# First mixture of experts of a four-layer decoder in blocks of 128 rows, with the rows as the stationary operand, four weight buffers and eight PSUM banks

## The chip, the cores and the metric

The kernel is one program on one core of a Trainium2 chip. The metric is device time in microseconds, the median of three runs. The profile and the trace are from one further execution.

## The reference, cut to what matters

A decoder of four layers works on x of 8 x 256 tokens with 256 features (2048 tokens, f32). Twelve stages follow one another; ten of them are not touched in their arithmetic or their order. The stage that is rewritten is the feed-forward part of layer 0, a mixture of 8 experts of which each token takes two:

```python
logits = jnp.einsum('th,eh->te', xf, w_router)
topw, topi = jax.lax.top_k(jax.nn.softmax(logits, axis=-1), 2)
topw = topw / jnp.sum(topw, axis=-1, keepdims=True)
gate = jax.nn.silu(jnp.einsum('th,eih->eti', xf, w_gate))   # 8 experts, i = 704, h = 256
up = jnp.einsum('th,eih->eti', xf, w_up)
down = jnp.einsum('eti,ehi->eth', gate * up, w_down)
out = jnp.einsum('eth,te->th', down, combine)               # combine holds topw at topi
```

A second stage matters for one part of the change: the self-attention of layer 3, which has a learned score for each distance between two tokens.

## The kernel before

Each stage is a class, and emits its whole instruction order for the five queues (PE, ACT, DVE, POOL, SP). An engine's queue runs in the order in which it is written; every wait is a semaphore wait in that order. `Uses` hands out PSUM banks (8 banks of 512 f32 columns) in rotation: `take` makes PE wait until the bank's last contents were copied out. By default it rotates over banks 0 to 5. Banks 6 and 7 are used by `Norm` for the turned activations (L389 to L405) of the next stage, four groups of four tiles each, whose transposes are issued while the present stage ends.

**The mixture, `L0Mixture`.** The router picks two experts for each token, which gives 4096 rows. Rows of one expert are put into blocks of BLOCK = 256 rows, no block holds two experts, and the program runs the largest number of blocks that can be needed: (4096 + 8 x 255) // 256 = 23. Empty places in a block are computed all the same; the scatter leaves them out. For block j:

- SP reads the expert's number and loads its whole weights (gate, up and down, 128 partitions x 4352 f32, 2176 KB) into one of RING = 3 buffers (L1357 to L1362). The load of block j waits for the last product of block j - 3.
- POOL gathers the rows with two indirect DMAs of 128 rows (L1169), into one of two buffers.
- PE turns the rows (`pe_turn`, 4 transposes), multiplies gate and up, 6 tiles of the 704 hidden features, with weights as the stationary operand and 256 rows as the moving one (24 products, L221), turns the rows of block j + 1, and then makes the down product of block j (12 products, L1283). An f32 product shows as two instructions.
- For each tile ACT takes silu of gate (L1298) and DVE multiplies by up (L1326), which gives the hidden features already turned as the down product wants them. ACT copies the result out (L1304), and POOL scatters it with two indirect DMAs (L1176).

The order on POOL is what sets when rows arrive:

```python
def pool(self):
    self.load_rows(0)
    self.load_rows(1)
    for j in range(BLOCKS):
        self.load_rows(j + 2)
        pool.wait_ge(*self.uses.emptied(self.y_use[j]))
        ...  # scatter of block j
```

So the gather of block j + 3 comes behind the scatter of block j in POOL's queue, and that scatter waits for the copy of the down product of block j.

**The distances in `L3Attention`.** For 8 batches, 2 tiles and 2 halves of the features (32 areas) PE makes 4 products into 4 banks (L2858), DVE and ACT copy two banks each (L236, L231) into one of 4 slots, and SP stores the slot to DRAM as `positions` (L2928): 1024 KB for each of 16 areas, 512 KB for each of the other 16, 25.2 MB in all. A slot is written again when its store has landed. When all are stored, SP loads the positions back (L2920), skewed; PE goes on with the queries and values and needs the first of them at the attention's first score.

Of the kernel before, what the change touches and what calls it, by code (L numbers as in the profile page):

```python
# [17 lines left out]
P = 128  # L18
# [9 lines left out]
BLOCK = 256  # L28
# [60 lines left out]
class Uses:  # L89
# [4 lines left out]
    def __init__(self, k, first=0, count=6):  # L94
        self.k, self.first, self.count, self.at = k, first, count, 0
        self.table, self.counts = [], {"dve": 0, "act": 0, "sums": 0}
# [1118 lines left out]
class L0Mixture(Mixture):  # L1215


    RING = 3

    def __init__(self, k):  # L1220
# [3 lines left out]
        MT = self.MT = tiles_of(I)  # L1224
        self.BT = BLOCK // P
# [4 lines left out]
        s4, s5, s6 = k.slab[4], k.slab[5], k.slab[6]  # L1230
        self.rows = [s4[:, 512 * n:512 * n + 512].rearrange("p (a c) -> p a c", a=2) for n in range(2)]
        self.rowsT = [s4[:, 1024 + 512 * n:1536 + 512 * n].rearrange("p (c t) -> p c t", c=DC) for n in range(2)]
        self.y = [s4[:, 2048 + 512 * n:2560 + 512 * n].rearrange("p (a c) -> p a c", a=2) for n in range(2)]
        self.silu = [s4[:, 3072 + 256 * n:3328 + 256 * n] for n in range(4)]
        self.hid = [s[:, 0:MT * BLOCK].rearrange("p (m t) -> p m t", m=MT) for s in (s5, s6)]
# [14 lines left out]
        self.rows_shared(self.BT, BLOCKS)  # L1250

    def pe_turn(self, j):
        k, nc, use = self.k, self.k.nc, self.uses
        if j < BLOCKS:
            k.pe.wait_ge(*self.rows_in(j))
            bank = use.take(self.turn[j])
            for c in range(DC):
                for a in range(2):
                    t = nc.tensor.transpose(bank[:, BLOCK * c + P * a:BLOCK * c + P * a + P],
                                            self.rows[j % 2][:, a, P * c:P * c + P], k.ident)  # L1260
# [2189 lines left out]
```

## Time and profile before

| what | value |
|---|---|
| median of 3 runs | 2955.96 us (2955.13 to 2957.3) |
| the profiled execution, its time | 2950.55 us |
| its span from first to last instruction | 2949.3 us |
| mean granted TensorE clock | 0.917 |
| PE busy | 2515.4 us, 85% of the span |
| mixture of layer 0, from the first gate product to the last down product | 257.46 to 651.30 us |
| distances of layer 3, from the first product to the first query product | 2215.33 to 2288.55 us |

A granted clock of 1.00 is 2.4 GHz, one of 0.50 is 1.2 GHz. Times in the rows are microseconds from the start of the span. The span leaves out what lies around it, 1.25 us in the profiled execution.

### The profile page before, as it was taken

Reading aid. Unit: us, or ns where it says so; the run is one execution under the profiler, and the core shown is the slowest. Engines: PE = TensorE matmul, PEld = TensorE weight load, DVE = VectorE, ACT = ScalarE, POOL = GpSimd, SP = SyncE. Lnnn points to the kernel's source line nnn. Section 1 sums busy time; section 2 is a strip of 40 time slices with the busy share of each in tenths; the row PEclk is TensorE's granted clock in tenths of the full one; section 3 lists DMA queues with packets and bytes.
Section 4 is the critical chain, followed back from the end, with each engine's and each line's share of the span. In section 5 each row is a group of like instructions: output and inputs, shape, how many; then the busy total and the mean of one; then the engine's idle time right before and its main releaser. Section 6 shows DMA issues by size and latency. Waiting matters only on the chain.

```text
span 2949.3 us, 34538 instructions
## 1 busy us (share of the span) xinstructions
PE 2515.4 (85%) x13798; PEld 1737.2 (59%) x13798; DVE 1221.9 (41%) x2235; ACT 870.2 (30%) x2379; POOL 570.1 (19%) x566
## 2 busy tenths in 40 slices
PE   4876999985899587887899999699956999867999
PEld 4764777764676363423566667577732788733555
DVE  6553111118588563556233321300044355665220
ACT  1110111113475161454222221122213344313220
POOL 2521222215201001211344310222220100012000
PEclk8977999997999798998899999699976999988999
DMA  4003443422001000300000000323227323100000
GB/s 149 1 29 139 174 160 145 169 79 78 1 2 48 0 2 0 119 1 29 1 0 0 1 1 14 110 83 96 71 88 313 158 87 130 37 25 0 8 8 15
DMA packets 73751, 189.50 MB, mean 64 GB/s; under 512 B 9551, under 2 KB 52949, under 8 KB 65654
## 3 DMA queue, kind: packets, MB, share of 16 engines
q1 hardware_dynamic: 65590, 169.11, 15.9%
q0 software_dynamic: 8000, 18.18, 1.9%
q8 instruction: 109, 1.79, 0.3%
q14 instruction: 52, 0.43, 0.0%
HBM read 143.88 MB, written 46.09 MB: 64 GB/s over the span
## 4 chain that ended last, share of the span: by engine, by line
PE 49%; DVE 6%; issue 1%; ACT 1%; POOL 1%; DMA 1%; SPq 0%; POOLq 0%; DVEq 0%; ACTq 0%
PE psum L221 25%; PE psum L3140 6%; PE psum L1685 3%; PE psum L2183 2%; PE psum L2170 2%; PE psum L3149 2%; PE psum L1680 2%; PE psum L2858 1%; PE psum L1696 1%; PE psum L1711 1%; DVE stats L253 1%; DVE arena L2230 1%; PE psum L2400 1%; POOL small L2598 1%; PE psum L404 1%
## 5 line engine op out<-in xcount | busy, mean ns | idle before, releaser
L221 PE MATMUL psum<-arena 128*128 128x256 f32 (+6 forms) x4112 | 994.3, 401 | 24.7 <-DVE arena L3236 13.5
L221 PEld LDWEIGHTS psum<-arena 128*128 128x128 f32 (+3 forms) x4112 | 718.9, 182 | 288.4 <-issue 147.4
L1770 DVE TENSOR_REDUCE small<-psum 128x4 f32<-128x1024 f32 (+1 forms) x112 | 137.0, 1223 | 152.8 <-PE psum L1685 108.6
L263 POOL TENSOR_SCALAR x_moments<-x_moments 128x4 f32<-128x4 f32 x48 | 12.0, 250 | 942.0 <-DVE x_moments L256 941.5
L1326 DVE TENSOR_TENSOR arena<-arena,psum 128x256 f32<-128x256 f32 x138 | 57.9, 420 | 317.7 <-ACT arena L1298 316.4
L1176 POOL DMA_INDIRECT l_out<-arena,slot_tables x86 | 85.6, 995 | 496.8 <-ACT arena L1304 287.8
L3140 PE MATMUL psum<-arena 128*128 128x512 bf16 x768 | 166.4, 379 | 0.0
L1745 ACT ACTIVATE arena<-psum,small 128x128 f32<-128x128 f32 (+1 forms) x384 | 148.9, 417 | 46.0 <-DVE small L1770 46.0
L1781 DVE COPY arena<-psum 128x512 f32<-128x512 f32 x224 | 143.5, 681 | 1.7 <-PE psum L1696 1.5
L404 PE MATMUL psum<-ident,z 128*128 128x128 f32 x256 | 47.0, 345 | 109.1 <-DVE z L274 79.7
L1745 ACT ACTIVATE z<-psum,small 128x128 f32<-128x128 f32 (+1 forms) x256 | 103.8, 425 | 117.6 <-DVE small L1770 117.6
L1283 PE MATMUL psum<-arena 128*128 128x256 f32 x552 | 136.5, 392 | 0.0
L1680 PE MATMUL psum<-arena 32*128 32x128 f32 (+1 forms) x1280 | 131.4, 336 | 0.0
L3140 PEld LDWEIGHTS psum<-arena 128*128 128x128 bf16 x768 | 75.2, 98 | 90.5
L2598 POOL TENSOR_TENSOR small<-small,minus_half 128x16 f32<-128x16 f32 x32 | 92.8, 2901 | 179.5 <-DVE small L2512 179.5
L221 PE MATMUL psum<-zT,arena 128*128 128x512 f32 x240 | 112.9, 625 | 7.2 <-DVE zT L234 5.7
L1283 PEld LDWEIGHTS psum<-arena 128*128 128x128 f32 x552 | 97.2, 189 | 32.8 <-issue 23.3
L2728 ACT ACTIVATE arena<-psum,small 128x269 f32<-128x269 f32 x128 | 61.4, 485 | 184.1 <-PE psum L221 171.8
L330 ACT ACTIVATE z<-x,x_shift,x_moments 128x256 f32<-128x256 f32 x96 | 52.2, 593 | 213.6 <-POOL x_shift L271 213.5
L1680 PEld LDWEIGHTS psum<-arena 32*128 32x128 f32 x1280 | 92.5, 189 | 38.6 <-issue 35.2
L221 PE MATMUL psum<-arena,zT 128*128 128x8 f32 (+2 forms) x384 | 108.6, 433 | 5.9 <-ACT zT L230 3.2
L1298 ACT ACTIVATE arena<-psum 128x256 f32<-128x256 f32 x138 | 52.7, 382 | 199.3 <-PE psum L221 197.9
(332 smaller groups left out, 3554.9 us busy)
## 6 DMA issues: line engine op xcount, KB each, us to landing
arena<-L_ffn_w_in SPq DMA_DIRECT2D x23, 2176.0 KB, 9.0
arena<-L_ffn_W_in SPq DMA_DIRECT2D x16, 1024.0 KB
positions<-arena SPq DMA_DIRECT2D x16, 1024.0 KB, 4.0
arena<-positions SPq DMA_DIRECT2D x16, 1024.0 KB, 7.9
arena<-l_out SPq DMA_DIRECT2D x16, 512.0 KB, 8.3
positions<-arena SPq DMA_DIRECT2D x16, 512.0 KB, 4.6
arena<-positions SPq DMA_DIRECT2D x16, 512.0 KB, 8.7
l_out<-arena SPq DMA_DIRECT2D x2, 2048.0 KB, 14.0
```

The source lines that it names most:

```text
L221: last = nc.tensor.matmul(out, lhsT, rhs, start=(n == 0), stop=(n == len(pairs) - 1))
L404: t = nc.tensor.transpose(bank[:, P * j:P * j + P], src[:, P * c:P * c + P], k.ident)
L1176: k.nc.gpsimd.indirect_dma_start(out=dram[:, :], out_offset=bass.IndirectOffsetOnAxis(ap=self.router.choice[0:count, n:n + 1], axis=0), in ...
L1283: mm = nc.tensor.matmul(bank[:, D * a:D * a + D], self.hid[j % 2][0:M, m, P * a:P * a + P], self.down[j % self.RING][0:M, m, :], start=(m ...
L1680: mm = nc.tensor.matmul(bank[:, at:at + L], self.q[p][strip, c, P * t:P * t + P], self.kT[strip, c, P * keys[0]:P * keys[0] + L], start=Fa ...
L1685: mm = nc.tensor.matmul(bank[:, at + P * a:at + P * a + P], self.positions(t, a, head), k.ident, start=False, stop=True, skip_group_check= ...
L1745: e = nc.scalar.activation(buf[:, at:at + L], src[:, at:at + L], ACT.Exp, bias=self.minus_top(h)[:, i:i + 1], scale=1.0, accum_out=self.su ...
L1770: nc.vector.reduce_max(self.minus_top(h), use.bank(u).rearrange("p (h l) -> p h l", l=L), AX_X, negate=True).then_inc(self.topped.up(), 1)
L1781: nc.vector.tensor_copy(self.turned[h % 4][:, 512 * s:512 * s + 512], use.bank(u)).then_inc(use.empties(u), 1)
L2598: k.nc.gpsimd.tensor_tensor(inv, inv, k.minus_half, ALU.pow).then_inc(self.inverted.up(), 1)
L2728: nc.scalar.activation(self.hid[e % 2][:, m, span], use.bank(u)[:, 0:self.half], ACT.Gelu, bias=self.b1[:, e, m:m + 1]).then_inc(use.empti ...
L3140: mm = nc.tensor.matmul(bank, self.w1[:, c, P * m:P * m + P], p[:, c, :], start=(c == 0 and n == 0), stop=(c == MT - 1 and n == 2))
```

## The change

The blocks of the first mixture have 128 rows, so there are (4096 + 8 x 127) // 128 = 39. For gate and up the turned rows are the stationary operand and 352 of the 704 weight columns the moving one: two halves of 4 products each, gate in one bank and up in the next. The hidden features come out with a row on each partition, so they are turned by 6 more transposes (`pe_hidden`), copied out by ACT (4 tiles) and DVE (2 tiles), and only then are they the stationary operand of the down product (6 products). The PE order is shifted: in its iteration j it makes the first half of block j, turns the hidden features of block j - 1, makes the second half of j, turns the rows of block j + 1, and makes the down product of j - 1. A block has one gather and one scatter in place of two each. There are four weight buffers. `Uses` rotates over all eight banks by default, in every stage that names no banks of its own (the cosine stage of layer 2 did already).

```diff
@@ -25,7 +25,7 @@
 LN_EPS = 1e-5
 SLAB = 4096
 ARENA = 9 * SLAB - 1024
-BLOCK = 256
+BLOCK = 128
 BLOCKS = (2 * TILES * P + E * (BLOCK - 1)) // BLOCK
 CAPACITY = int(round(2 * TILES * P * 1.05 / E))
 
@@ -91,7 +91,7 @@
 
 
 
-    def __init__(self, k, first=0, count=6):
+    def __init__(self, k, first=0, count=8):
         self.k, self.first, self.count, self.at = k, first, count, 0
         self.table, self.counts = [], {"dve": 0, "act": 0, "sums": 0}
 
@@ -1215,39 +1215,54 @@
 class L0Mixture(Mixture):
 
 
-    RING = 3
+
+
+    RING, HALVES = 4, 2
 
     def __init__(self, k):
         self.k = k
         cols = self.cols = k.d["L0_ffn_w"].shape[2]
         I = self.I = next(n for n in range(cols) if 2 * DC * n + tiles_of(n) * D == cols)
-        MT = self.MT = tiles_of(I)
-        self.BT = BLOCK // P
+        MT, half = tiles_of(I), I // self.HALVES
+        self.MT, self.half = MT, half
         self.wbuf = [k.arena[:, cols * n:cols * n + cols] for n in range(self.RING)]
...
+        at = cols * self.RING
+        self.rows, self.y = ([k.arena[:, at + D * n:at + D * n + D] for n in (m, m + 1)] for m in (0, 2))
+        at += 4 * D
+        self.rowsT = [k.arena[:, at + D * n:at + D * n + D].rearrange("p (c t) -> p c t", c=DC) for n in range(2)]
+        at += 2 * D
+        self.silu = [k.arena[:, at + half * n:at + half * n + half] for n in range(4)]
+        at += 4 * half
+        self.hid = [k.arena[:, at + I * n:at + I * n + I] for n in range(2)]
+        at += 2 * I
+        self.hidT = [k.arena[:, at + P * MT * n:at + P * MT * n + P * MT].rearrange("p (m t) -> p m t", m=MT) for n in range(2)]
...
-        self.router = Router(k, u, self.norm, self.fetch.loaded, BLOCKS * self.BT, None, True)
-        self.turn, self.gu, self.y_use = [u.add("dve")], [], []
-        for j in range(BLOCKS):
-            self.gu.append([u.add("dve") for _ in range(MT)])
-            if j + 1 < BLOCKS:
-                self.turn.append(u.add("dve"))
-            self.y_use.append(u.add("act"))
+        self.router = Router(k, u, self.norm, self.fetch.loaded, BLOCKS, None, True)
+        self.turn, self.gu, self.hid_use, self.y_use = [u.add("dve")], [], [], []
+        for j in range(BLOCKS + 1):
+            if j < BLOCKS:
+                self.gu.append([u.add("dve", 2)])
+            if j:
+                self.hid_use.append([u.add("act"), u.add("dve")])
+            if j < BLOCKS:
+                self.gu[j].append(u.add("dve", 2))
+                if j + 1 < BLOCKS:
+                    self.turn.append(u.add("dve"))
+            if j:
+                self.y_use.append(u.add("act"))
         u.close()
-        self.silu_in = k.counter("silu_written", "act").reserve(BLOCKS * MT)
+        self.silu_in = k.counter("silu_written", "act").reserve(BLOCKS * self.HALVES)
...
+    def pe_half(self, j, n):
+        bank, at = self.uses.take(self.gu[j][n]), self.half * n
+        for i, w in enumerate((self.gate[j % self.RING], self.up[j % self.RING])):
+            mm = products(self.k.nc, bank[:, 512 * i:512 * i + self.half],
+                          [(self.rowsT[j % 2][:, c, :], w[:, c, at:at + self.half]) for c in range(DC)])
+        mm.then_inc(self.uses.fills(self.gu[j][n]), 1)
+
+    def pe_hidden(self, j):
+        k, nc, use = self.k, self.k.nc, self.uses
+        k.pe.wait_ge(*use.emptied(self.gu[j][-1]))
+        for n, u in enumerate(self.hid_use[j]):
+            bank = use.take(u)
+            for m in range(4 * n, min(4 * n + 4, self.MT)):
+                at, M = P * (m % 4), self.rows_of(m)
+                t = nc.tensor.transpose(bank[0:M, at:at + P], self.hid[j % 2][:, P * m:P * m + M], k.ident)
+            t.then_inc(use.fills(u), 1)
+
+    def pe_out(self, j):
+        k, nc, use = self.k, self.k.nc, self.uses
+        for u in self.hid_use[j]:
+            k.pe.wait_ge(*use.emptied(u))
+        bank = use.take(self.y_use[j])
+        products(nc, bank[:, 0:D], [(self.hidT[j % 2][0:self.rows_of(m), m, :], self.down[j % self.RING][0:self.rows_of(m), m, :])
+                                    for m in range(self.MT)]).then_inc(use.fills(self.y_use[j]), 1)
+
     def pe(self):
-        k, nc, pe, use, I = self.k, self.k.nc, self.k.pe, self.uses, self.I
+        pe, use = self.k.pe, self.uses
         self.router.pe()
         self.pe_turn(0)
-        for j in range(BLOCKS):
-            pe.wait_ge(self.ring[j % self.RING], j // self.RING + 1)
-            pe.wait_ge(*use.emptied(self.turn[j]))
-            for m, u in enumerate(self.gu[j]):
-                M = min(P, I - P * m)
-                bank = use.take(u)
-                for n, w in enumerate((self.gate[j % self.RING], self.up[j % self.RING])):
-                    mm = products(nc, bank[0:M, BLOCK * n:BLOCK * n + BLOCK],
-                                  [(w[:, c, P * m:P * m + M], self.rowsT[j % 2][:, c, :]) for c in range(DC)])
-                mm.then_inc(use.fills(u), 1)
-            self.pe_turn(j + 1)
-            bank = use.take(self.y_use[j])
-            for a in range(self.BT):
-                for m in range(self.MT):
-                    pe.wait_ge(*use.emptied(self.gu[j][m]))
-                    M = min(P, I - P * m)
-                    mm = nc.tensor.matmul(bank[:, D * a:D * a + D], self.hid[j % 2][0:M, m, P * a:P * a + P],
-                                          self.down[j % self.RING][0:M, m, :], start=(m == 0), stop=(m == self.MT - 1))
-            mm.then_inc(use.fills(self.y_use[j]), 1)
+        for j in range(BLOCKS + 1):
+            if j < BLOCKS:
+                pe.wait_ge(self.ring[j % self.RING], j // self.RING + 1)
+                pe.wait_ge(*use.emptied(self.turn[j]))
+                self.pe_half(j, 0)
+            if j:
+                self.pe_hidden(j - 1)
+            if j < BLOCKS:
+                self.pe_half(j, 1)
+                self.pe_turn(j + 1)
+            if j:
+                self.pe_out(j - 1)
...
     def act(self):
...
+        for j in range(BLOCKS + 1):
+            if j < BLOCKS:
+                self.act_silu(j, 0)
+            if j:
+                u = self.hid_use[j - 1][0]
                 act.wait_ge(*use.filled(u))
-                if n >= 4:
-                    act.wait_ge(*use.emptied(gu[n - 4]))
-                nc.scalar.activation(self.silu[n % 4][0:M], use.bank(u)[0:M, 0:BLOCK],
-                                     ACT.Silu).then_inc(self.silu_in.up(), 1)
-            u = self.y_use[j]
-            act.wait_ge(*use.filled(u))
-            if j >= 2:
-                act.wait_ge(*self.y_out(j - 2))
-            nc.scalar.copy(self.y[j % 2], use.bank(u).rearrange("p (a c) -> p a c", a=2)).then_inc(use.empties(u), 1)
+                if j >= 3:
+                    act.wait_ge(*use.filled(self.y_use[j - 3]))
+                nc.scalar.copy(self.hidT[(j - 1) % 2][:, 0:4, :],
+                               use.bank(u).rearrange("p (m t) -> p m t", m=4)).then_inc(use.empties(u), 1)
+            if j < BLOCKS:
+                self.act_silu(j, 1)
+            if j:
+                u = self.y_use[j - 1]
+                act.wait_ge(*use.filled(u))
+                if j >= 3:
+                    act.wait_ge(*self.y_out(j - 3))
+                nc.scalar.copy(self.y[(j - 1) % 2], use.bank(u)[:, 0:D]).then_inc(use.empties(u), 1)
...
             u = self.turn[j]
             k.dve.wait_ge(*use.filled(u))
+            if j >= 2:
+                k.dve.wait_ge(*use.filled(self.gu[j - 2][-1]))
             k.nc.vector.tensor_copy(self.rowsT[j % 2],
-                                    use.bank(u).rearrange("p (c t) -> p c t", c=DC)).then_inc(use.empties(u), 1)
+                                    use.bank(u)[:, 0:D].rearrange("p (c t) -> p c t", c=DC)).then_inc(use.empties(u), 1)
+
+    def dve_half(self, j, n):
+        dve, use, u, at = self.k.dve, self.uses, self.gu[j][n], self.half * n
+        dve.wait_ge(self.silu_in, self.HALVES * j + n + 1)
+        dve.wait_ge(*use.filled(u))
+        if j >= 2:
+            dve.wait_ge(*use.filled(self.hid_use[j - 2][-1]))
+        self.k.nc.vector.tensor_tensor(self.hid[j % 2][:, at:at + self.half], self.silu[(self.HALVES * j + n) % 4],
+                                       use.bank(u)[:, 512:512 + self.half], ALU.mult).then_inc(use.empties(u), 1)
 
...
     def load_rows(self, j):
@@ -1335,8 +1394,7 @@
             else:
                 self.k.pool.wait_ge(self.z_stored)
                 self.k.pool.wait_ge(*self.router.tokens_in())
-            for a in range(self.BT):
-                self.gather(j, self.rows[j % 2][:, a, :], self.BT * j + a)
+            self.gather(j, self.rows[j % 2], j)
 
     def pool(self):
         pool = self.k.pool
@@ -1346,8 +1404,7 @@
             self.load_rows(j + 2)
             pool.wait_ge(*self.uses.emptied(self.y_use[j]))
             pool.wait_ge(*self.router.choices_in())
-            for a in range(self.BT):
-                self.scatter(j, self.k.l0_out, self.y[j % 2][:, a, :], self.BT * j + a)
+            self.scatter(j, self.k.l0_out, self.y[j % 2], j)
         self.finals("pool")
 
...
@@ -2297,7 +2354,7 @@
         self.hid = [s[n].rearrange("p (m t) -> p m t", m=MT) for n in (3, 1)]
         self.ctx_moments, self.own = Moments(k, "own", self.ctx, k.own_moments), Moments(k, "own", k.z, k.own_moments)
 
-        u = self.uses = Uses(k, count=8)
+        u = self.uses = Uses(k)
         self.ctx_turn = Turn(k, u, self.normed, self.cT, TILES, scale=g1, bias=b1n)
         self.k_use, self.v_use, self.q_use, self.kv_use, self.qT_use, self.oT_use = [], [], [], [], [], []
         self.wo_use, self.turn_use, self.h_use, self.out_use = [], [], [], []
```

## Rows read from the trace of the kernel before

**Rows 1.** Windows, mixture: length, then busy PE PEld DVE ACT POOL, clock, DMA share, GB/s.
```profile
261.00:652.00 391.00, 390.30 (x1737) 300.45 (x1735) 71.14 (x160) 66.20 (x161) 85.58 (x84) 1.00 0.39 139
```

**Rows 2.** Timeline, one block: start, us, engine, line, instruction, [idle before].
```profile
276.36 10.77 PE L221 MATMUL psum<-arena 128*128 128x256 f32 x48
...
287.06 0.66 PE L1259 MATMUL psum<-ident,arena 128*128 128x128 f32 x4
...
287.56 5.93 PE L1283 MATMUL psum<-arena 128*128 128x256 f32 x24
...
293.42 10.77 PE L221 MATMUL psum<-arena 128*128 128x256 f32 x48
293.53 0.58 ACT L1304 COPY arena<-psum 128x512 f32<-128x512 f32 x1 [5.98 <-PE psum L1283]
294.91 1.02 POOL L1176 DMA_INDIRECT l_out<-arena,slot_tables  x1 [12.06 <-ACT arena L1304]
...
297.54 1.05 POOL L1169 DMA_INDIRECT arena<-z_rows,slot_tables  x1 [0.30 <-issue]
```

**Rows 3.** Timeline, same block: ACT and DVE on one tile.
```profile
278.39 0.38 ACT L1298 ACTIVATE arena<-psum 128x256 f32<-128x256 f32 x1 [1.34 <-PE psum L221]
...
278.81 0.42 DVE L1326 TENSOR_TENSOR arena<-arena,psum 128x256 f32<-128x256 f32 x1 [7.27 <-ACT arena L1298]
```

**Rows 4.** DMA queues, windows from 293.42, 295.92, 298.92 and 301.42: packets, MB, share.
```profile
q1 hardware_dynamic: 14, 0.24, 48.4%
...
q1 hardware_dynamic: 57, 0.99, 88.5%
...
q1 hardware_dynamic: 53, 0.92, 91.5%
q0 software_dynamic: 32, 0.11, 11.2%
...
q0 software_dynamic: 160, 0.41, 41.1%
```

**Rows 5.** Timeline, first rows of layer 2's mixture, no weight load running.
```profile
1880.86 0.95 POOL L1169 DMA_INDIRECT arena<-z_rows,slot_tables  x1 [0.31 <-issue]
...
1883.30 2.62 PE L2680 MATMUL psum<-ident,arena 128*128 128x128 f32 x10 [9.86 <-DMA arena<-z_rows,slot_tables]
```

**Rows 6.** Chain of waits, layer 2's cosine stage: start, us, what.
```profile
1496.99 17.34 PE psum L221 x80
```

**Rows 7.** Timeline of PE, convolution stage of layer 3: gaps and what follows.
```profile
2597.79 5.42 PE L221 MATMUL psum<-arena,inverse 128*128 128x512 f32 x12 [2.11 <-DVE arena L3030]
...
2609.67 7.06 PE L221 MATMUL psum<-arena,inverse 128*128 128x512 f32 x12 [3.03 <-DVE arena L3030]
...
2623.83 6.80 PE L221 MATMUL psum<-arena,inverse 128*128 128x512 f32 x12 [3.67 <-DVE arena L3030]
...
2638.34 5.42 PE L221 MATMUL psum<-arena,inverse 128*128 128x512 f32 x12 [3.39 <-DVE arena L3030]
```

**Rows 8.** Window of the distances of layer 3, columns as in rows 1.
```profile
2230.00:2235.00 5.00, 2.38 (x24) 0.89 (x16) 2.58 (x4) 2.17 (x4) 0.00 (x0) 0.91 1.02 414
```

**Rows 9.** Timeline of the distances: first products, a later wait, first query product, first load.
```profile
2215.33 1.14 PE L2858 MATMUL psum<-arena 32*128 32x512 f32 x8
...
2241.43 2.09 PE L2858 MATMUL psum<-arena 32*128 32x512 f32 x8 [1.01 <-DVE arena L236]
...
2288.55 15.78 PE L221 MATMUL psum<-zT,arena 128*128 128x512 f32 x32
...
2293.71 4.19 SPq L2920 DMA_DIRECT2D arena<-positions  x8
```

**Rows 10.** Timeline, end of layer 1's attention: last products, first turned group.
```profile
944.57 3.62 PE L221 MATMUL psum<-arena,zT 128*128 128x256 f32 x16
...
947.17 0.69 DVE L234 COPY zT<-psum 128x512 f32<-128x512 f32 x1
...
947.77 1.28 DVE L486 TENSOR_TENSOR x<-x,psum 128x512 f32<-128x512 f32 x2
```

More of the change, by code:

```diff
@@ L1229, in __init__ @@
         self.down = [w[:, 2 * DC * I:cols].rearrange("p (m n) -> p m n", m=MT) for w in self.wbuf]
[L1230 to L1235, printed above, removed]
+        at = cols * self.RING
[8 more added lines that the diff above has]
+        self.hidT = [k.arena[:, at + P * MT * n:at + P * MT * n + P * MT].rearrange("p (m t) -> p m t", m=MT) for n in range(2)]
         self.fetch = Fetch(k, (k.slab[8][:, 1536:1552].rearrange("p (c e) -> p c e", c=DC),
@@ L1239, in __init__, with rows_of @@
         u = self.uses = Uses(k)
-        self.router = Router(k, u, self.norm, self.fetch.loaded, BLOCKS * self.BT, None, True)
-        self.turn, self.gu, self.y_use = [u.add("dve")], [], []
-        for j in range(BLOCKS):
-            self.gu.append([u.add("dve") for _ in range(MT)])
-            if j + 1 < BLOCKS:
-                self.turn.append(u.add("dve"))
-            self.y_use.append(u.add("act"))
+        self.router = Router(k, u, self.norm, self.fetch.loaded, BLOCKS, None, True)
[11 more added lines that the diff above has]
+                self.y_use.append(u.add("act"))
         u.close()
-        self.silu_in = k.counter("silu_written", "act").reserve(BLOCKS * MT)
+        self.silu_in = k.counter("silu_written", "act").reserve(BLOCKS * self.HALVES)
         self.ring = [k.loads(f"expert_weights{n}", len(range(n, BLOCKS, self.RING))) for n in range(self.RING)]
-        self.rows_shared(self.BT, BLOCKS)
+        self.rows_shared(1, BLOCKS)
+    def rows_of(self, m):
+        return min(P, self.I - P * m)
     def pe_turn(self, j):
@@ L1257, in pe_turn @@
             for c in range(DC):
-                for a in range(2):
-                    t = nc.tensor.transpose(bank[:, BLOCK * c + P * a:BLOCK * c + P * a + P],
-                                            self.rows[j % 2][:, a, P * c:P * c + P], k.ident)
+                t = nc.tensor.transpose(bank[:, P * c:P * c + P], self.rows[j % 2][:, P * c:P * c + P], k.ident)
             t.then_inc(use.fills(self.turn[j]), 1)
+    def pe_half(self, j, n):
[4 more added lines that the diff above has]
+        mm.then_inc(self.uses.fills(self.gu[j][n]), 1)
@@ L1286, in pe, with act_silu @@
-        self.finals("pe")
+        for j in range(BLOCKS + 1):
[10 more added lines that the diff above has]
+                self.pe_out(j - 1)
+        self.finals("pe")
+    def act_silu(self, j, n):
+        k, act, use = self.k, self.k.act, self.uses
+        u, h = self.gu[j][n], self.HALVES * j + n
+        act.wait_ge(*use.filled(u))
+        if j >= 2:
+            act.wait_ge(*use.emptied(self.gu[j - 2][n]))
+        k.nc.scalar.activation(self.silu[h % 4], use.bank(u)[:, 0:self.half], ACT.Silu).then_inc(self.silu_in.up(), 1)
@@ L1290, in act @@
         self.router.act()
-        gu = [u for us in self.gu for u in us]
-        for j in range(BLOCKS):
-            for m, u in enumerate(self.gu[j]):
-                M, n = min(P, self.I - P * m), self.MT * j + m
-                act.wait_ge(*use.filled(u))
-                if n >= 4:
-                    act.wait_ge(*use.emptied(gu[n - 4]))
-                nc.scalar.activation(self.silu[n % 4][0:M], use.bank(u)[0:M, 0:BLOCK],
-                                     ACT.Silu).then_inc(self.silu_in.up(), 1)
-            u = self.y_use[j]
-            act.wait_ge(*use.filled(u))
-            if j >= 2:
-                act.wait_ge(*self.y_out(j - 2))
-            nc.scalar.copy(self.y[j % 2], use.bank(u).rearrange("p (a c) -> p a c", a=2)).then_inc(use.empties(u), 1)
+        for j in range(BLOCKS + 1):
[3 more added lines that the diff above has]
+                u = self.hid_use[j - 1][0]
+                act.wait_ge(*use.filled(u))
+                if j >= 3:
[6 more added lines that the diff above has]
+                u = self.y_use[j - 1]
+                act.wait_ge(*use.filled(u))
+                if j >= 3:
+                    act.wait_ge(*self.y_out(j - 3))
+                nc.scalar.copy(self.y[(j - 1) % 2], use.bank(u)[:, 0:D]).then_inc(use.empties(u), 1)
         self.finals("act")
@@ L1318, in dve @@
         self.dve_turn(0)
-        for j in range(BLOCKS):
-            for m, u in enumerate(self.gu[j]):
-                M, n = min(P, self.I - P * m), self.MT * j + m
-                dve.wait_ge(self.silu_in, n + 1)
-                dve.wait_ge(*use.filled(u))
-                if m == 0 and j >= 2:
-                    dve.wait_ge(*use.filled(self.y_use[j - 2]))
-                nc.vector.tensor_tensor(self.hid[j % 2][0:M, m, :], self.silu[n % 4][0:M],
-                                        use.bank(u)[0:M, BLOCK:2 * BLOCK], ALU.mult).then_inc(use.empties(u), 1)
-            self.dve_turn(j + 1)
+        for j in range(BLOCKS + 1):
+            if j < BLOCKS:
+                self.dve_half(j, 0)
+            if j:
+                u = self.hid_use[j - 1][1]
+                dve.wait_ge(*use.filled(u))
+                if j >= 3:
+                    dve.wait_ge(*use.filled(self.y_use[j - 3]))
+                for m in range(4, self.MT):
+                    M, at = self.rows_of(m), P * (m - 4)
+                    last = nc.vector.tensor_copy(self.hidT[(j - 1) % 2][0:M, m, :], use.bank(u)[0:M, at:at + P])
+                last.then_inc(use.empties(u), 1)
+            if j < BLOCKS:
+                self.dve_half(j, 1)
+                self.dve_turn(j + 1)
         self.dve_combine()
```

1 line of the change is left out of this document (added).

## Prediction

> **What bounds the kernel now.** I read the windows of the mixture first. Between 261 and 652 us PE is busy for 390.30 of 391.00 us at a granted clock of 1.00, which is 2.4 GHz; DVE, ACT and POOL are busy for under a quarter each, and the DMA engines for 0.39 of the time [rows 1]. So this stage is as long as PE's work, and the reader is to see that nobody else is near. The timeline of one block comes next: gate and up begin at 276.36, the row transposes at 287.06, the down products at 287.56, the next block at 293.42. A block is 17.06 us and 23 blocks are 392.4 us [rows 2]. Then I looked at what runs beside PE and costs nothing today: the rows and the weights. From the end of a block's down product at 293.42, called T here, the scatter starts on POOL at T + 1.49, the gather at T + 4.12 [rows 2]; the rows that it brings are turned only two blocks on, some 25 us later. The DMA queues by window show what happens meanwhile: the weight load (q1) begins inside the first window, and the rows' queue (q0) moves nothing before 298.92, T + 5.5, though the scatter left POOL at T + 2.51. It moves 32 of its 192 packets until T + 8.0, while q1 runs, and 160 in the window after it, in which q1 has few left [rows 4]. Rows in effect wait for the weights. Last, I looked at the other stages for waits on banks; one of them stands out, the distances of layer 3.
>
> **PE's own work per block.** A 256-column instruction takes 17.34 / 80 = 0.217 us [rows 6], one of 512 columns 5.42 / 12 = 0.452 [rows 7]; between them one of 352 columns takes 0.217 + 96 x 0.235 / 256 = 0.305. Eight gate and up products are 16 instructions, 4.88 us, or 2.44 a half. Transposes take (287.56 - 287.06) / 4 = 0.125, so 6 + 2 take 1.00. The down products took 5.86 for 24 instructions [rows 2]; 12 take 2.93. That is 8.81 us a block, and 343.6 for 39: 48.8 less than 392.4. The blocks that fall away (39 x 128 rows against 23 x 256) pay for more than the new transposes.
>
> **ACT and DVE** have for a block two silus, copies of 512 and 256 columns, two products, three copies. The nearest rows are 0.38 and 0.42 for 256 columns [rows 3] and 0.58 for 512 [rows 2]; at 0.6 for each of the nine it is under 3 us on either engine, beside 8.81 of PE. The order on PE puts 2.93 + 2.44 us between the last half and its transposes, and 2.44 between the transposes and the down product, against 0.38 + 0.42 and 0.58: free. If that cover went, it would be 0.5 us a block.
>
> **Weights.** 39 loads of 2.23 MB in place of 23. A load has 128 packets, and q1 moves 53 in a window of 2.5 us with 0.915 of the engines [rows 4], so 5.5 to 6.6 us a load with its slow start, under 8.81. With four buffers it is issued two iterations ahead. Bandwidth is not the bound. At the start a fourth load delays the first rows by 0 to 3 us; I take 0.
>
> **The gather, which is moved.** POOL's queue is untouched: scatter j, then gather j + 3. But the down product of block j now ends one iteration later, at the start T of iteration j + 2, and `pe_turn(j + 3)` stands in that same iteration. The path from T: ACT's copy starts 0.11 later and is 0.20 shorter than before (256 columns), so the scatter starts at T + 1.29, ends at T + 2.31, and the gather runs from T + 2.61 to T + 3.66 [rows 2, 3]. SP issues a weight load at the same T, as today. PE gets to `pe_turn` at T + 2.44 + 0.75 + 2.44 = T + 5.63, and it waits there in order: the down product behind it, which starts the next round, waits too.
> How long does the gather take from POOL's end? Without a weight load 1.49 us (1881.81 to 1883.30) [rows 5]: T + 5.15, no wait. With one, today's 192 packets are served as above; the new block has 96, of the same two kinds at the same places. 32 are moved by T + 8.0, and the other 64 at 64 a us: T + 9.0, and some 0.3 earlier since q1 is disturbed by half as many [rows 4]. I take rows turned from T + 8.8. From below: T + 7.9, when q1 is through. From above: T + 9.6, where today's last would be at half of the last window's tail. So the wait is 3.17 us a block (2.3 to 4.0). It is paid where scatter, gather and a weight load meet, iterations 2 to 36, 35 times: 111 us (80 to 140).
>
> **The clock.** Gaps of this size are in the trace: after one of 2.11 us twelve products took 5.42, after 3.03 they took 7.06, after 3.67 6.80, after 3.39 5.42 [rows 7]. The three of 3 us and more cost 1.64, 1.38 and 0, on average 1.0, and here the work behind the gap is the down product that the next round waits for. 35 x 1.0 = 35 us (0 to 52).
>
> **Eight banks elsewhere.** In the distances of layer 3 an area takes four banks, so with six PE waits for copies each time (1.01 us idle and then 2.09 of products at the low clock) [rows 9]. With eight, two areas alternate. What bounds it then is the store: 25.2 MB at 414 GB/s, with the DMA engines already full in such a window [rows 8], take 60.8 us, and landing and start 4 more: the last store is in at 2280, where it is now at 2293.71, and PE can go to the queries when all but the last four areas are stored, at about 2273 in place of 2288.55 [rows 9]. The queries hide the rest. I take 14 us off (between 5, if the stores don't stay packed, and 16). Against it: bank 6 and 7 now also hold other uses. At the end of layer 1's attention the seventh pair of the last product would sit in bank 6 behind the copy of zT, which runs from 947.17, where PE did it from 944.57 [rows 10]: 3 us, and some 1 more at the end of the stage after it (0 to 6 together). Net -10.
>
> **The sum**, against the profiled execution: 2950.55 - 48.8 + 111 + 35 - 10 = 3037.8. The median of the runs stands 5.4 above that execution: 3043.
>
> **Rivals.**
> *Rows come in time.* If the gather gets its turn beside the weights, it lands at T + 5.15 and nothing waits. Then it is -48.8 - 10, so 2897. For it: the light case [rows 5], and DMA engines at 0.39 [rows 1]. Against it: no packet of q0 before T + 5.5 today [rows 4]. It decides if rows are there by T + 5.6.
> The Trainium skill (DMA: Bandwidth & Descriptors, Queues, rings and completion order) says that an engine goes round between its queues packet by packet, which is this rival's reason; its fixed 2.0 us for a DMA (the same page, Anatomy of one DMA) would give a landing, an estimate, at T + 2.61 + 2.3, and no wait. This case's trace has the first packet of q0 3 us after POOL was through, so I go by the trace.
> *A short wait.* Rows at T + 7.0 to 7.5, with no loss of clock: 1.4 to 1.9 us a block, 49 to 66 us, against -59: within 10 us of no change. It needs q0 served faster than in any window with q1.
> *The clock stays low.* If the gap brings PE to 1.2 GHz for most of an iteration, halves and transposes take 11.3 us and the down product 5.9; at half of the iterations this adds about 70 us: 3110. For it: the stage of the distances, at the low clock with 1 us gaps. Against: [rows 7], where it comes back after a few us.
> That the change doesn't do what it says is no rival for the blocks; for the banks it is the 5 us bound above.
>
> **How the numbers follow.** The long wait 0.70, with its own range 2980 (T + 7.9, no loss of clock) to 3090 (T + 9.6 and 1.5 of clock); clock low 0.07; short wait 0.10, half of it above no change; rows in time 0.13. A measurement of this kernel tells a change from none from about 0.2%. Slower 0.70 + 0.07 + 0.03 = 0.80, same 0.04, faster 0.16. The range 2945 to 3090 leaves out the rows in time and the low clock.
>
> **What would show it.** Right: the row transposes (the two per block, on ident and rows) wait on the gather's DMA about 35 times for 2.5 to 4 us; a block of 11.5 to 13.5 us; the granted clock below 1.00 in the stage; q0 served only when q1 ends. The distances some 14 us shorter with full DMA. Wrong: blocks of 9 us with PE busy throughout (rows in time), or a wait on weights (their bandwidth was mis-sized).

## The result, and the profile after

The changed kernel takes 3118.75 us (median of 4 runs, 3116.59 to 3127.06) against 2956.63 of the kernel before beside it: a ratio of 1.0555, 95% interval 1.0543 to 1.0567. It is slower by 162 us; the forecast was 3043, its range ended at 3090. So the direction was right, and the size was too small by 76 us.

From the windows of the changed kernel (columns as in [rows 1]): the stage from the first long wait for rows in the steady state to the last, then 5.92 us behind the wait of one iteration, then the start of that iteration, ahead of its wait.

```profile
289.14:799.32 510.18, 368.52 (x1225) 245.31 (x1225) 63.19 (x170) 63.26 (x136) 69.65 (x68) 0.84 0.45 166
349.69:355.61 5.92, 5.92 (x14) 4.02 (x15) 0.42 (x1) 0.00 (x0) 0.00 (x0) 0.52 0.00 0
340.00:345.50 5.50, 5.50 (x22) 3.45 (x22) 0.91 (x3) 1.39 (x3) 2.04 (x2) 1.00 0.73 234
```

PE was busy for all of the stage [rows 1]; now it is for 368.5 of 510.2 us, at a granted clock of 0.84. Behind the wait the clock is 0.52, hence 1.2 GHz nearly throughout, and ahead of it 1.00. The timeline shows an iteration, from the copy of a down product to the next down product:

```profile
339.99 0.37 ACT L1347 COPY arena<-psum 128x256 f32<-128x256 f32 x1 [8.78 <-PE psum L221]
...
341.16 1.01 POOL L1176 DMA_INDIRECT l_out<-arena,slot_tables  x1 [12.47 <-ACT arena L1347]
...
342.48 1.03 POOL L1169 DMA_INDIRECT arena<-z_rows,slot_tables  x1 [0.30 <-issue]
...
343.01 2.53 PE L221 MATMUL psum<-arena 128*128 128x352 f32 x8
...
349.69 0.69 PE L1273 MATMUL psum<-ident,arena 128*128 128x128 f32 x2 [4.15 <-DMA arena<-z_rows,slot_tables]
...
350.18 8.07 PE L221 MATMUL psum<-arena 128*128 128x256 f32 x20
```

T, the end of the down product, is 0.11 us before the copy, at 339.88. The scatter starts at T + 1.28, the gather runs from T + 2.60 to T + 3.63, PE is through with its second half at T + 5.66, all as forecast. The rows are there at T + 9.81, where T + 8.8 was forecast. The last line joins the 12 instructions of the down product and the 8 of the next half; unhindered these 20 are shown with 5.51 us, and behind the 35 waits of this size with 6.64 to 8.20. The list of waits has 37 for rows: the first of 9.54, one of 0.63, and 35 of 3.66 to 5.07 whose mean is (155.9 - 9.54 - 0.63) / 35 = 4.16:

```profile
PE psum L1273 <- DMA arena<-z_rows,slot_tables: 155.9, 37, 9.5
```

The queues of the same iteration, in windows of 2.5 us from T on, answer to [rows 4]:

```profile
q1 hardware_dynamic: 16, 0.28, 57.3%
...
q1 hardware_dynamic: 44, 0.77, 78.5%
...
q1 hardware_dynamic: 52, 0.91, 87.4%
q0 software_dynamic: 26, 0.10, 9.6%
...
q1 hardware_dynamic: 32, 0.28, 26.3%
q0 software_dynamic: 70, 0.16, 16.6%
```

q0 carries the scatter and the gather, 96 packets a block. In windows of half a microsecond the first of them moves between T + 5.5 and T + 6.0; 36 have moved by T + 8.0, beside q1's, and the other 60 as q1 ends. In the distances of layer 3 eight banks did what was expected; here is the window from their first product to the first query product:

```profile
2397.09:2455.91 58.82, 37.59 (x258) 16.08 (x257) 31.43 (x62) 27.83 (x63) 0.00 (x0) 0.73 0.96 391
```

58.8 us in place of 73.2 [rows 9], with the DMA engines at 0.96. And a loss that nobody looked for is in the first stage, before the mixture:

```profile
67.95 2.47 PE L221 MATMUL psum<-fourier,arena 128*128 128x256 f32 x5 [14.29 <-DVE arena L703]
```

### The profile page after: what moved, and what is told of

Its sections match the earlier page's. It is cut to its first block, busy times and chain, and to the rows that moved or that the text cites. A ratio compares the mean times of both kernels' runs of the same rounds, so it can differ in the third digit from the quotient of the medians.

```text
span 3118.7 us, 33870 instructions
## 1 busy us (share of the span) xinstructions
PE 2538.3 (81%) x13454; PEld 1713.5 (55%) x13454; DVE 1221.8 (39%) x2269; ACT 877.6 (28%) x2374; POOL 557.1 (18%) x552
## 4 chain that ended last, share of the span: by engine, by line
PE 45%; DVE 6%; DMA 2%; ACT 1%; POOL 1%; issue 1%; SPq 0%; POOLq 0%; DVEq 0%; ACTq 0%
PE psum L221 24%; PE psum L3197 5%; PE psum L1742 3%; PE psum L2240 2%; PE psum L3206 2%; PE psum L2227 2%; PE psum L1737 2%; DMA positions<-arena 1%; PE psum L1753 1%; DVE stats L253 1%; PE psum L1768 1%; DVE arena L2287 1%; PE psum L2457 1%; POOL small L2655 1%; PE psum L404 1%
## 5 line engine op out<-in xcount | busy, mean ns | idle before, releaser
L221 PE MATMUL psum<-arena 128*128 128x256 f32 (+6 forms) x4100 | 1126.3, 433 | 26.0 <-DVE arena L3293 13.0
L221 PEld LDWEIGHTS psum<-arena 128*128 128x128 f32 (+2 forms) x4100 | 762.4, 195 | 349.3 <-issue 167.9
L1176 POOL DMA_INDIRECT l_out<-arena,slot_tables x79 | 78.9, 999 | 677.5 <-ACT arena L1347 469.8
L1366 DVE TENSOR_TENSOR arena<-arena,psum 128x352 f32<-128x352 f32 x78 | 40.7, 522 | 354.5 <-ACT arena L1325 354.5
L1273 PE MATMUL psum<-ident,arena 128*128 128x128 f32 x78 | 24.0, 406 | 155.9 <-DMA arena<-z_rows,slot_tables 155.9
L1273 PEld LDWEIGHTS psum<-ident,arena 128*128 128x128 f32 x78 | 10.4, 184 | 176.8 <-DMA arena<-z_rows,slot_tables 176.2
L1347 ACT COPY arena<-psum 128x256 f32<-128x256 f32 x39 | 14.5, 373 | 324.3 <-PE psum L221 324.3
```

The source lines that it names most:

```text
L221: last = nc.tensor.matmul(out, lhsT, rhs, start=(n == 0), stop=(n == len(pairs) - 1))
L1176: k.nc.gpsimd.indirect_dma_start(out=dram[:, :], out_offset=bass.IndirectOffsetOnAxis(ap=self.router.choice[0:count, n:n + 1], axis=0), in ...
```

## The experiments

All times are medians. Each ratio is to the kernel before on the same chip, with its 95% interval; the runs below were made on four chips, on which the kernel before took 2957.37 to 2963.01 us, so the ratios compare better than the times do. T is in each the end of a block's down product.

**Eight banks alone.** The kernel before with `count=8` in place of `count=6`.

> The kernel before with eight banks by default and nothing else changed. The comparison of the two traces by PE's instructions says that eight banks cost 6 us in the first stage (the next stage's first product waits for a late bank), 6 to 7 in layer 1's attention, 3 before the last stage, and give 14 in the distances of layer 3: about +1 us in all, 2955 to 2960. The prediction's own step said 10 us less: 2947.

2949.46 us, 0.9972 (0.9962 to 0.9981): 8 us faster. The expectation from the traces (+1) was wrong; much of the cause was the trace it was compared with:

**The kernel before once more**, for a second trace.

> The kernel before once more, for its trace: the one at hand was of an execution 5 to 7 us below the median of all runs. Where this one is later than it, differences between the traces of before and of other kernels are no effect of a change. With eight banks alone the trace was 10 us behind in layer 1's attention; if that is the banks, this trace agrees with the first there, within 1 us.

Its span is 2960.2 us, 10.9 more than that of the first, with the same code. It is 3.7 behind the first in layer 1's attention, where agreement within 1 us was expected, 5.2 in the distances of layer 3 (78.4 for 73.2, at a granted clock of 0.53 for 0.63), and some 4 in the rest of layer 3. Against this trace, eight banks alone cost 7.7 us in the first stage and 5.5 in layer 1's attention, and give 20.5 in the distances (57.9); the remaining 4 of the 11.3 us between the spans lie in other stages. The timeline has the wait of the second stage's first products, with eight banks and then, in a fence of its own, in the kernel before:

```profile
68.64 1.62 PE L221 MATMUL psum<-fourier,arena 128*128 128x256 f32 x3 [13.99 <-DVE arena L703]
```

```profile
60.94 9.24 PE L221 MATMUL psum<-fourier,arena 128*128 128x256 f32 x34 [7.55 <-DVE arena L703]
```

The first stage has 17 uses of banks. Over six, the last falls in bank 4, and bank 0, which the next stage takes first, is free after the fourth of eight attention outputs. Over eight, the seventeenth falls in bank 0 itself, and the next stage waits for the last output's reader on DVE.

**The gather ahead of the scatter**, all else as changed.

```diff
-        self.load_rows(0)
-        self.load_rows(1)
+        for n in range(3):
+            self.load_rows(n)
         for j in range(BLOCKS):
-            self.load_rows(j + 2)
+            self.load_rows(j + 3)
             pool.wait_ge(*self.uses.emptied(self.y_use[j]))
```

> The changed kernel, with the gather of block j + 3 issued ahead of the scatter of block j on POOL. If the late rows are the whole loss, PE never waits in the middle of the stage, a block is 8.7 to 8.8 us, the clock is 1.00, and the time is 2900 to 2912 (39 x 8.75 = 341 in place of 564 us). Rival, weights: each load takes 8.9 us from issue to landing in the changed kernel; if that is their real rate, blocks are 9 to 10 us with waits on the weights, 2915 to 2955. Rival, rows slow by themselves: no change from 3119.

2888.49 us, 0.9768 (0.9753 to 0.9783), 11.5 us below the expected range; half of that is the block of 8.60 us where the expectation took 8.75. This one swap takes off 230 us. Five lines of its PE timeline span a whole block (the first and the last are the same transposes, of two blocks):

```profile
310.71 0.38 PE L1273 MATMUL psum<-ident,arena 128*128 128x128 f32 x2
...
310.93 5.51 PE L221 MATMUL psum<-arena 128*128 128x256 f32 x20
...
316.28 0.82 PE L1290 MATMUL psum<-ident,arena 128*128 128x128 f32 x6
...
316.94 2.53 PE L221 MATMUL psum<-arena 128*128 128x352 f32 x8
...
319.31 0.38 PE L1273 MATMUL psum<-ident,arena 128*128 128x128 f32 x2
```

A block is 319.31 - 310.71 = 8.60 us without a wait. The rivals fall: the weights keep up, and the rows are slow only if they are needed in the iteration that asks for them.

**Weights loaded for four blocks only**: `if j >= self.RING: continue` ahead of the load, and PE waits for the first load of each buffer alone. The later blocks are computed with the weights that lie in the buffers.

> The changed kernel, which loads the expert weights of the first four blocks only (the later ones are left out, their products are made with the weights in the buffers), so that no weight load runs beside a gather; the order on POOL is that of the changed kernel. If only the load starves the gather, rows are there at T + 5.1 to T + 5.5, blocks take 8.6 us, and the time is that of the gather put first, 2885 to 2900. If the gather behind the scatter is late by itself, it stays above 3000.

2899.09 us, 0.9797 (0.9780 to 0.9814), with POOL's order as changed. Behind the first wait the list has eight for rows, of 0.19 to 0.65 us, 3.4 us together; in the iteration looked at the rows are turned at T + 5.5. The queue in the 2.5 us from T to T + 2.5 is empty but for one packet of instructions, and the next window has

```profile
q0 software_dynamic: 94, 0.26, 32.5%
```

so 94 of 96 packets move between T + 2.5 and T + 5.0, where in the changed kernel none did. Taken in halves of a microsecond they come as two lots of 48: the scatter's up to T + 3.5, the gather's from T + 4.0. So the scatter too is held up by a load, and the gather's packets, which are in the same queue, come behind it.

**Weight loads issued behind the row transposes**, the same bytes at another time:

```diff
                 sp.wait_ge(*self.uses.filled(self.y_use[j - self.RING]))
+                sp.wait_ge(*self.uses.filled(self.turn[j - 1]))
```

> The changed kernel, its order on POOL kept, but a weight load is issued only once PE has turned the rows of that iteration, so gather and load no longer start together. If the load starves the gather, rows land at T + 5.1 to T + 5.5, PE waits 0 to 0.5 us a block, and the time is 2900 to 2925. If the gather behind the scatter is late by itself, rows stay near T + 9.8, and the time is 3110 to 3130. If half of each, 3000 to 3050.

2957.30 us, 1.0000 (0.9991 to 1.0010): 162 us less than the changed kernel and 69 more than the one with the gather first, and in none of the ranges that were expected. The list has 32 waits for rows; without the first of 9.5 they are 1.6 us each. The timeline tells why:

```profile
317.16 0.44 PE L1273 MATMUL psum<-ident,arena 128*128 128x128 f32 x2 [2.35 <-DMA arena<-z_rows,slot_tables]
...
320.42 0.37 ACT L1347 COPY arena<-psum 128x256 f32<-128x256 f32 x1 [5.11 <-PE psum L221]
321.60 1.01 POOL L1176 DMA_INDIRECT l_out<-arena,slot_tables  x1 [8.80 <-ACT arena L1347]
322.91 1.03 POOL L1169 DMA_INDIRECT arena<-z_rows,slot_tables  x1 [0.30 <-issue]
...
328.43 0.44 PE L1273 MATMUL psum<-ident,arena 128*128 128x128 f32 x2 [2.46 <-DMA arena<-z_rows,slot_tables]
```

The load is now issued at 318.41, behind the transposes of 317.16, and still runs when the gather is issued; with T at 320.31, q0 gets all but one of its 96 packets from T + 5.0 on, as q1 ends: 80 of them have moved by T + 6.5, the last 16 take until T + 8.0. Rows come at 328.43, T + 8.1. From issue to landing a load takes 8.9 us in the changed kernel, more than the 8.6 that a block has; there is hardly a place in the iteration where the gather would meet none.

**Products in the gap.** Seven more products (`FILL = 7`) before `pe_turn`, into the bank that the down product overwrites; the lines that hand out that bank are left out here.

```diff
+                if 2 <= j <= BLOCKS - 4:
+                    self.pe_fill(j, FILL)
                 self.pe_turn(j + 1)
```

> The changed kernel, with seven more products (3.4 us, a result that the down product overwrites) in front of the row transposes in iterations 2 to 35: they fill the wait of 4.16 us. If the 2.1 us a block that the iteration loses behind the wait come from the clock that falls in it, a block is 12.9 us, and the time 75 us less than the changed kernel's: 3044 (3035 to 3055). If they have another cause (buffers, banks), it stays at 3110 to 3125.

3055.28 us, 1.0330 (1.0313 to 1.0346): 63.5 us faster than the changed kernel, with more work on PE.

```profile
311.33 3.19 PE L1305 MATMUL psum<-arena 128*128 128x256 f32 x14
...
316.38 0.44 PE L1274 MATMUL psum<-ident,arena 128*128 128x128 f32 x2 [1.86 <-DMA arena<-z_rows,slot_tables]
...
316.65 5.51 PE L222 MATMUL psum<-arena 128*128 128x256 f32 x20
```

The 20 instructions behind the wait take 5.51 again, and the granted clock from 290.11 to 725.23 is 1.00. A block is 13.19 us ((725.23 - 290.11) / 33), against 15.01 in the changed kernel ((799.32 - 289.14) / 34). The 1.82 us between them are the clock's: the rows still come at T + 9.8 on average (5.40 + 3.05 of fill + a mean wait of 1.33). The expected 3044 took all 2.1 us that lay behind the wait as the clock's.

**No shift.** The down product of block j in iteration j again, behind its hidden transposes.

```diff
-        for j in range(BLOCKS + 1):
...
-            if j:
-                self.pe_out(j - 1)
+        for j in range(BLOCKS):
...
+            self.pe_half(j, 0)
+            self.pe_half(j, 1)
+            self.pe_turn(j + 1)
+            self.pe_hidden(j)
+            self.pe_out(j)
```

> The changed kernel with its down product in the same iteration again: two halves, the next rows' transposes, the hidden transposes, the down product. The gather then has an iteration more, so PE does not wait for rows. Instead the hidden transposes wait for the last silu and product (0.2 + 0.47 + 0.52 us, less 0.22 of row transposes, so 1.0) and the down product for the copies (0.8): 8.6 + 1.8 = 10.4 us a block, 39 x 10.4 = 406, and 2888 + 70 = 2958 (2945 to 2975, the upper end if such gaps lower the clock). If the shift is not why rows are late, waits for rows of 4 us remain, and it is over 3100.

2969.56 us, 1.0029 (1.0016 to 1.0042), in the expected range. No wait for rows but the first; the two expected ones stand in their place, 0.89 and 0.66 us:

```profile
313.19 0.38 PE L1268 MATMUL psum<-ident,arena 128*128 128x128 f32 x2
...
314.46 0.87 PE L1285 MATMUL psum<-ident,arena 128*128 128x128 f32 x6 [0.89 <-DVE arena L1353]
...
316.00 0.45 PE L221 MATMUL psum<-arena 128*128 128x256 f32 x1 [0.66 <-DVE arena L1370]
```

A block is 10.60 us. The granted clock is 1.00 in an iteration with these short gaps.

**Blocks of 128 and nothing else.** `BLOCK = 128` in the kernel before: weights stationary, three buffers, six banks.

> The kernel before with blocks of 128 rows and nothing else changed: weights stationary, three buffers, six banks. If an instruction of 128 columns takes as long as a transpose (0.11 to 0.125), 48 of them and the 2.98 of the down product and 0.22 make 8.5 to 9.2 us, and the rows as the stationary operand bring nothing: 2890 to 2925. If the loads of stationary tiles bound it (0.17 to 0.20 each, as PEld shows them), a block is 11.4 to 12.8 us and the time 3005 to 3060. With three buffers a load of 8.9 us has one iteration, so a block is no shorter than 8.9.

2907.14 us, 0.9820 (0.9804 to 0.9837), so faster than before by 54 us.

```profile
301.56 5.75 PE L221 MATMUL psum<-arena 128*128 128x128 f32 x48
...
307.24 0.44 PE L1259 MATMUL psum<-ident,arena 128*128 128x128 f32 x2
...
307.51 2.95 PE L1283 MATMUL psum<-arena 128*128 128x256 f32 x12
...
310.39 5.75 PE L221 MATMUL psum<-arena 128*128 128x128 f32 x48
```

48 instructions of 128 columns take 5.68 us, 0.118 each, so the loads of stationary tiles (0.183 us each in the profile's list) don't bound it, and a block is 8.84. The down product is in its own iteration, the gather keeps an iteration of room, and PE is busy for 338.00 of 338.00 us between 262 and 600. Rows as the stationary operand are worth 8.84 - 8.60 = 0.24 us a block.

**Three buffers**: the gather first, `RING = 3`.

> The gather put first, with three weight buffers in place of four. A load then has one iteration of 8.6 us and takes 8.9 from issue to landing (with the rows of one gather beside it): PE waits 0.3 to 1 us a block on the weights, 12 to 40 us more than 2888, and if the short gaps lower the clock another 10 to 40. If loads land in 8.6 us when nothing is queued before them, no change: 2888.

2914.57 us, 0.9842 (0.9827 to 0.9858), 26 us more by the medians, 22 by the ratios. The list of waits has 27 of PE on weights, 19.3 us in all, here one of 0.65:

```profile
317.15 2.63 PE L221 MATMUL psum<-arena 128*128 128x352 f32 x8 [0.65 <-DMA arena<-L_ffn_w_in]
```

The two blocks around it are 9.23 us each on average. So the fourth buffer is needed, but only together with the shorter block and the shift.

**Smaller packets.** The load in 4 and in 2 transfers by columns, with 4.35 and 8.7 KB in a packet; order, shift and bytes as in the changed kernel.

> The changed kernel, its order kept, each weight load as four transfers of 1088 columns, so that its packets have 4.35 KB in place of 17.4 KB. Theory of turns: beside a load, q0 and q1 move about as many packets a us each (20 and 22), so each of the gather's 6 packets on an engine waits for one packet of q1; that is 0.76 us each with 17.4 KB, 4.6 us in all, and 0.19 each and 1.1 us in all with 4.35 KB. Rows then land near T + 6.3 in place of T + 9.8, PE waits 0.5 to 1 us a block, and the time is 2905 to 2945. Theory of order: the gather is served only when the load before it is through, whatever its packets; rows stay at T + 9.8 and the time at 3110 to 3130.

> The same with two transfers of 2176 columns, packets of 8.7 KB. Theory of turns: 0.38 us a packet, 2.3 us in all, rows near T + 7.5, a wait of 1.9 us a block and some clock: 2960 to 3020. Theory of order: 3110 to 3130.

3080.21 us, 1.0420 (1.0402 to 1.0439), and 3098.19 us, 1.0475 (1.0456 to 1.0494). Both theories fall as they were put. Mean waits are 3.42 and 3.71 us in place of 4.16, so rows come at about T + 9.1 and T + 9.4: the size of the packets matters, but for 0.7 us, not for 3.5. The microsecond from T + 6 to T + 7 with parts of a quarter, and then in the changed kernel:

```profile
q1 hardware_dynamic: 76, 0.31, 75.8%
q0 software_dynamic: 41, 0.11, 26.7%
...
q1 hardware_dynamic: 20, 0.35, 81.6%
q0 software_dynamic: 14, 0.06, 13.9%
```

Here q0 moves 41 packets in place of 14, and with the small ones 91 of its 96 are through by T + 8.0 (36 in the changed kernel). But the last five take until the load ends, near T + 9, and the rows are turned only behind them, at T + 9.2. And its first packet comes between T + 5.5 and T + 6.0 at every size, 3 us later than without a load (T + 2.5 to T + 3.0). What holds up that first packet is not settled.

**The choice of banks.** The gather first, with six banks again in the first stage, in both stages of layer 1 up to its attention, and in layer 3's convolution; and the kernel before with blocks of 128 and the same banks.

> The changed kernel with the gather ahead of the scatter, and six banks again in the first stage, in both stages of layer 1 up to its attention and in the convolution of layer 3. From the traces, eight banks cost 7 us in the first stage and 5 in layer 1's attention and gain in the distances: 2888 less 12, so 2876 (2870 to 2882). If the banks of these stages don't matter, it stays at 2888.

> The kernel before with blocks of 128 rows and the same choice of banks as the run beside it: weights stationary, three buffers, down product in its own iteration. The stage took 5.9 us longer in its trace than in that of the gather put first, so 6 us above the run beside it: 2882 (2876 to 2888). If the rows as the stationary operand are worth their 0.24 us a block and more, 9 to 12 above it.

2879.57 us, 0.9721 (0.9708 to 0.9734), the fastest of all; and 2886.61 us, 0.9751 (0.9737 to 0.9765). By the ratios, 0.47%, 14 us, are gained on the changed form, where four stages go from eight banks back to six, and 0.69%, 20 us, on the old one, where all other stages go from six to eight. The two differ from each other by 0.30%, 9 us, which is what 39 blocks of 0.24 us make. Of the four stages that went back to six, none was run apart, and only the first was looked at by its wait.

## Why the prediction was wrong

*PE's work* was right: 8.81 us forecast, 8.60 measured. The view of half and transposes was right to 0.1 us, and PE alone would have taken 39 x 0.21 = 8 us less than the sum has. *ACT and DVE* were right. *The weights* were right in that with four buffers nobody waits for them; but a load was put at 5.5 to 6.6 us, and its packets move from T + 1.5 to T + 9, before and after alike.

*The gather, which is moved*, was the right mechanism, in the right place, as often as forecast (35 times). It needs all three: the shift, the order on POOL, and the weight load. Take away any one of the three and the wait is gone, but for 3.4 us in all in the last of these runs (2969.56 us, 2888.49, 2899.09). Its size was too small: rows at T + 9.8, beyond the upper bound of T + 9.6, for T + 8.8. The step that failed is "the other 64 at 64 a us: T + 9.0, and some 0.3 earlier". The 64 a us is the mean of a window of 2.5 us [rows 4] with 160 packets. In halves of a microsecond from T + 8.0 on, these 160 are 19, 61, 53, 23 and 4: a slow start beside the end of q1, a peak, and a tail. The first two of them:

```profile
q0 software_dynamic: 19, 0.05, 26.5%
...
q0 software_dynamic: 61, 0.16, 81.9%
```

In the changed kernel there are three such halves:

```profile
q0 software_dynamic: 23, 0.06, 28.8%
...
q0 software_dynamic: 28, 0.07, 35.0%
...
q0 software_dynamic: 9, 0.02, 8.5%
```

and none after T + 9.5. With fewer packets the peak is missing; start and tail stay. So the queue is through near T + 9.4 in place of T + 9.0. The credit of 0.3 for a less disturbed q1 didn't exist: q1 has moved 124 packets by T + 8.0 in both kernels. And from the last packet to the transposes another 0.4 us pass, where the forecast had 0.1. Together this is 1.0 us a block, 35 us. The lower bound of T + 7.9, "when q1 is through", was no bound either: q1 still moves packets after T + 8.0, before and after.

*The clock* was the other miss. The forecast had 1.0 us a block, and the filled gap shows 1.82: 64 us for 35, above even the upper bound of 1.5. The step "the three of 3 us and more cost 1.64, 1.38 and 0, on average 1.0" put in the mean a gap that cost nothing [rows 7]. Here each of the 35 gaps is followed by slow work, and with 4.16 us they are on average longer than any of those. The rival "the clock stays low" had 70 us more for the clock than the forecast, 105 in all, and got 0.07; the clock's 64 lie between the two. That its 3110 is near the measured time is luck: it had the waits 35 us too short.

In sum a block of the steady state took 15.01 us for 8.81 + 3.17 + 1.0 = 12.98. The 2.03 us between them are 1.0 of later rows, 0.8 of clock, and 0.4 more around each wait that no run splits further, less 0.2 of PE's work; 35 x 2.03 = 71 of the 76 us. The other 5 are less than two executions of one kernel differ by. The upper end of the range took both bounds at once and still was 0.7 a block short.

*Eight banks elsewhere* came out at -8 for -10, with parts that were wrong on both sides. The distances gave 14 against the trace of before and 20 against its second trace. The price was looked for at the end of layer 1's attention; the first stage, which costs 7 us, was not examined. The step that failed here is that only banks 6 and 7 were checked for other holders, not bank 0, where one stage hands over to the next.

*The rows come in time* had as its reason that an engine goes round between queues. By the runs the load does keep the rows' queue out until T + 5.5, and slows it after that. The Trainium skill (DMA: Bandwidth & Descriptors, Queues, rings and completion order) says more exactly that an engine drains a whole packet of several descriptors from one ring before it changes. The profile's "packets" are smaller pieces, 128 in a load and so 8 on each of 16 engines; if those 8 are one packet of the page, parts of a quarter should have let the rows' queue in far earlier than the whole load did. Its first packet came between T + 5.5 and T + 6.0 all the same, so no run here bears the rule out as the reason of the delay.

## What to carry to other kernels

Ask of a transfer that is hidden today in which iteration it is issued and in which it is needed, and redo that count when work is shifted by an iteration: here the shift took away the one iteration of room that the gather had, and swapping two lines of a queue gave 230 us back. Price a small gather beside a large load by the end of the load, and a gap of 4 us on PE with at least the highest loss of clock that shorter gaps show, not with their mean. Before more than one thing is changed, run the simplest part alone: blocks of 128 in the old form gave 54 of the 83 us that the fastest version found.

## What was not expected of the hardware

- A hardware queue's load delays the first packet of the software queue by 3 us (T + 5.5 for T + 2.5, in windows of 0.5), the same with packets of 17.4, 8.7 and 4.35 KB. Once both move, q0 gets more packets through in the same microsecond the smaller q1's are (14, 18 and 41), but its last packets still end with the load.
- Filling a wait on PE with useless products made the kernel 63.5 us faster, since the granted clock behind it stayed up.
- Two executions of the same kernel differed by 10.9 us in their traces, 5.2 of them in the distances of layer 3, where the granted clock was 0.63 in one and 0.53 in the other. A difference of some us in one stage needs a second trace of before.
